# State space phase: the preparation chain of a tile starts two steps earlier, and the gate z is made together with the next tile's conv

## Chip, core and metric

One core of a Trainium2 chip runs the whole kernel in one launch. The metric is the time on the device in microseconds (us) of one execution; the kernel is float32 with a few bf16 operands that stand for exact splits.

## What is computed

The input x is (8, 64, 128, 128). A first layer (attention over the 4096 pooled pixels of each image, layer norm, bilinear upsampling) gives an image of the same size. The second layer, where the change is, is a state space block over the pixels in raster order, all eight images as one sequence of 131072 tokens with 64 channels, 128 inner channels and 16 states:

```python
xz = u @ in_proj_w.T
xh, z = (xz[:, :d_inner], xz[:, d_inner:])
xp = jnp.pad(xh, ((D_CONV - 1, 0), (0, 0)))
conv = conv_b
for k in range(D_CONV):
    conv = conv + xp[k:k + L] * conv_w[:, k]
xc = jax.nn.silu(conv)
dbc = xc @ x_proj_w.T
dt = dbc[:, :dt_rank]
...
delta = jax.nn.softplus(dt @ dt_proj_w.T + dt_proj_b)
A = -jnp.exp(A_log)
def step(h, t):
    d, b, c, xt = t
    h = h * jnp.exp(d[:, None] * A) + (d * xt)[:, None] * b[None, :]
    return (h, h @ c)
...
y = ys + xc * D
y = y * jax.nn.silu(z)
```

Behind it stand two projections, a layer norm over the 64 channels, a silu and the residual sum with u.

## The kernel before

The program has two phases: `attention_phase`, which writes its tokens to `zn_tokens`, and `mamba_phase`, from about 4900 us of the profile on. Only the second is touched. It goes through 256 tiles of 512 tokens (TB), 128 channels on the partitions; state n of a tile is one [128, 512] row of work, and there are S = 16 of them. The order on each engine is written out by hand: a loop body of 16 steps, `step(n)` for n in 14, 15 of tile g and then for n in 0 to 13 of tile g + 1, two tiles (s = 0 and 1) to one pass of the inner loop. Engines meet only by semaphores, and each carries out its own list in order.

What one step holds on each engine:

- **VectorE**: `inputs(n + 1)`, the product of the next state's B row (in one of four PSUM banks `bbank`) with `du` (L904), then the scan of state n (L918).
- **TensorE**: `spread_b(n + 3)` writes the B row of state n + 3 into `bbank` (L1123; it needs the scan of four states earlier), then `add_state(n - 3)` adds a product with C into `ybank` (L1133, `sum_mm`; "add k" below). Step 3 has no add, and step 4 has the skip term (L1131) and adds 0 and 1.
- **ScalarE**: `decay(n + 4)`, the exponential `da` of one state (L1033).
- **GpSimd**: the product `pr` of state n with its C row (L838).

Beside it, `prep(n, tau)` prepares tile g + 2 in fixed steps, and `post(n, g)` finishes tile g. The chain of `prep`, with the step at which it stands before:

- TensorE 0: `ubank` <- u, the upsampling (L1078). ScalarE 1: two short copies of history and two copies of `ubank` to `u2` (L955 to L961).
- TensorE 2: conv, two matmuls into `vbank` (L1084, L1085), and z into `ubank` (L1087). ScalarE 3: `xc`, `sz` (the gate, which waits for `yb` of the tile that used its buffer), and `so` of an earlier tile (L967, L971, L1007), between two loads of an activation table.
- TensorE 5: `vbank` <- `xc` and `ubank` <- `xc` (L1091, L1093). ScalarE 6: `av`, `bcs` (the first part of B and C), `ev`, `ct`, `e1`, `lv`, `ed` (L977 to L993), ScalarE 7: relu (L995).
- TensorE 7: the first remainder, "neg" (L1097); ScalarE 8: `bcs` again (L998, signal `mid_done`; "mid"); TensorE 9: the second remainder, "last" (L1102, waits for `mid_done`); ScalarE 10: the low part (L1001).
- GpSimd 8, 9: `cv` and `l2` (L808, L813). VectorE 11: `dl` (L886), which the decays and `du` of that tile need. GpSimd 12: `du` (L817).

`post` holds: ScalarE 0 `ures` (L1014), VectorE 3 `yb` (L892, after the last add), TensorE 5 `pc` (L1109), ScalarE 6 `sl` (the square, L1018), TensorE 8 the variance (L1114), ScalarE 9 `lnr` and `rs`, VectorE 12 `qn` (L896), GpSimd 6 the residual (L829). On an engine that has both, ScalarE does `post` before `prep`, TensorE `prep` before `post`. SyncE writes the C rows of a tile to memory and loads them back spread over the partitions, and loads the tokens of later tiles.

## Time and profile before

| | us |
|---|---|
| median of 3 runs | 13125.51 (13124.51 to 13127.3) |
| the profiled execution | 13120.83 |
| span of its profile | 13119.0 |

| engine | busy us | share of the span |
|---|---|---|
| TensorE, matmul | 11668.5 | 89% |
| VectorE | 10235.9 | 78% |
| ScalarE | 7905.5 | 60% |
| GpSimd | 7307.1 | 56% |

The shares are means over both phases: in the first VectorE is half idle, and in the second it is over nine tenths busy. So only a view of the second phase tells what bounds it. Matmul ends in the trace are modelled, so that a busy TensorE is not one at its peak.

### The profile page before, as it was taken

Reading aid. Unit: us, or ns where it says so; the run is one execution under the profiler, and the core shown is the slowest. Engines: PE = TensorE matmul, PEld = TensorE weight load, DVE = VectorE, ACT = ScalarE, POOL = GpSimd, SP = SyncE. Lnnn points to the kernel's source line nnn. Section 1 sums busy time; section 2 is a strip of 40 time slices with the busy share of each in tenths; the row PEclk is TensorE's granted clock in tenths of the full one; section 3 lists DMA queues with packets and bytes.
Section 4 is the critical chain, followed back from the end, with each engine's and each line's share of the span. In section 5 each row is a group of like instructions: output and inputs, shape, how many; then the busy total and the mean of one; then the engine's idle time right before and its main releaser. Section 6 shows DMA issues by size and latency. Waiting matters only on the chain.

```text
span 13119.0 us, 161233 instructions
## 1 busy us (share of the span) xinstructions
PE 11668.5 (89%) x34287; PEld 4280.2 (33%) x34287; DVE 10235.9 (78%) x13211; ACT 7905.5 (60%) x12824; POOL 7307.1 (56%) x5412
## 2 busy tenths in 40 slices
PE   4989899999989998888888888888888888888888
PEld 1333333333333333333333333333333333333333
DVE  6454545455454439999999999999999999999999
ACT  1333333333333337777777777777777777777777
POOL 6030303022030007777777777777777777777777
PEclk9989899999989999999999999999999999999999
DMA  2010100101010003333333433333343343333333
GB/s 56 2 27 2 27 9 21 28 2 27 2 27 2 1 10 150 151 144 147 155 144 144 156 146 144 151 151 144 147 155 144 144 155 147 144 152 150 144 149 153
DMA packets 372433, 1297.68 MB, mean 99 GB/s; under 512 B 177904, under 2 KB 177904, under 8 KB 231792
## 3 DMA queue, kind: packets, MB, share of 16 engines
q1 hardware_dynamic: 372336, 1296.81, 26.8%
q14 instruction: 88, 0.72, 0.0%
q8 instruction: 9, 0.15, 0.0%
HBM read 1246.07 MB, written 50.56 MB: 99 GB/s over the span
## 4 chain that ended last, share of the span: by engine, by line
PE 22%; issue 15%; ACT 14%; DVE 9%; POOL 1%; ACTq 0%; DVEq 0%; POOLq 0%; DMA 0%; SPq 0%
PE ybank L1133 7%; ACT da L1033 6%; DVE bbank L904 5%; DVE h L918 3%; PE bbank L1123 2%; PE ubank L1087 2%; PE pbank L1109 2%; PE vbank L1084 2%; PE vbank L1085 2%; PE vbank L1091 2%; PE ubank L1093 2%; PE ybank L1131 2%; ACT av L977 1%; ACT e L989 1%; ACT ev L984 1%
## 5 line engine op out<-in xcount | busy, mean ns | idle before, releaser
L838 POOL TENSOR_TENSOR pr<-h,cc 128x512 f32<-128x512 f32 x4110 | 5201.5, 1269 | 1381.4 <-DVE h L918 1380.1
L918 DVE TENSOR_TENSOR_SCAN h<-da,h,bbank 128x512 f32<-128x512 f32 x4110 | 5198.8, 1265 | 0.0
L1133 PE MATMUL ybank<-pr,m_small 128*128 128x512 f32 x8214 | 4195.6, 597 | 0.0
L904 DVE TENSOR_TENSOR bbank<-bbank,du 128x512 f32<-128x512 f32 x4111 | 2766.5, 673 | 44.6 <-PE bbank L1123 10.0
L432 ACT ACTIVATE prob<-st 128x512 f32<-128x512 f32 x2048 | 1222.7, 597 | 2575.1 <-PE st L564 2575.1
L1033 ACT ACTIVATE da<-dl,a 128x512 f32<-128x512 f32 x4114 | 2736.4, 712 | 17.1 <-DVE dl L886 1.1
L307 DVE TENSOR_REDUCE mpart<-s 128x1 f32<-128x512 f32 x2048 | 1322.2, 686 | 1089.5 <-PE s L530 1081.0
L1123 PE MATMUL bbank<-bcs,selb 96*128 96x512 bf16 x4113 | 1556.5, 389 | 646.7 <-DVE h L918 623.9
L564 PE MATMUL st<-qf,kf 65*128 (+1 forms) x4096 | 2121.3, 620 | 5.9 <-ACT qf L436 5.9
L240 POOL TENSOR_TENSOR rowsum<-xin 128x1024 f32<-128x1024 f32 x64 | 153.5, 2398 | 2994.4 <-PE vb L597 2905.0
L1133 PEld LDWEIGHTS ybank<-pr,m_small 128*128 128x128 f32 x8214 | 1561.0, 194 | 678.7 <-issue 597.6
L1123 PEld LDWEIGHTS bbank<-bcs,selb 96*128 96x128 bf16 x4113 | 375.7, 96 | 2726.1 <-DVE h L918 2209.8
L808 POOL TENSOR_TENSOR cv<-ed,ev 128x512 f32<-128x512 f32 x258 | 327.2, 1268 | 1408.2 <-ACT ed L993 1407.9
L579 PE MATMUL ob<-prob,v 128*64 128x512 f32 x4096 | 1090.5, 616 | 0.0
L564 PEld LDWEIGHTS st<-qf,kf 65*128 65x128 f32 x4096 | 696.5, 190 | 1123.1 <-issue 617.8
L529 PE MATMUL s<-ka,qh 128*128 128x512 bf16 x2048 | 791.5, 386 | 134.6 <-DVE mpart L307 112.3
L530 PE MATMUL s<-ka,qm 128*128 128x512 bf16 x2048 | 787.4, 384 | 0.0
L958 ACT COPY u<-ubank 64x512 f32<-64x512 f32 x258 | 149.4, 579 | 1041.3 <-PE ubank L1078 1041.3
L337 DVE TENSOR_SCALAR zn<-z,mv,rstd 128x64 f32<-128x64 f32 x256 | 62.9, 310 | 912.4 <-ACT rstd L448 912.4
L1018 ACT ACTIVATE sl<-pbank,pbc 64x512 f32<-64x512 f32 x256 | 174.7, 682 | 578.8 <-PE pbank L1109 578.8
L300 DVE SCALAR_TENSOR_TENSOR yc<-xb,dwq,yc (+1 forms) x256 | 455.4, 1779 | 33.3 <-DVE yc L300 23.4
L886 DVE TENSOR_TENSOR dl<-l,vbank 128x512 f32<-128x512 f32 x258 | 177.6, 688 | 349.8 <-issue 330.5
(153 smaller groups left out, 11693.5 us busy)
## 6 DMA issues: line engine op xcount, KB each, us to landing
cc<-c_rows SPq DMA_DIRECT2D x1032, 1024.0 KB, 7.9
upw<-up SPq DMA_DIRECT2D x260, 256.0 KB, 9.5
xin<-x SPq DMA_DIRECT2D x128, 512.0 KB, 6.8
out<-ot SPq DMA_DIRECT2D x256, 128.0 KB, 2.3
zw<-zn_tokens SPq DMA_DIRECT2D x780, 32.0 KB, 9.8
c_rows<-crows SPq DMA_DIRECT2D x258, 32.0 KB, 1.6
zn_tokens<-znb SPq DMA_DIRECT2D x64, 128.0 KB, 2.0
a_small<-small SPq DMA_DIRECT2D x1, 1331.0 KB, 5.6
```

The costliest lines, as they stand in the source:

```text
L307: dve.tensor_reduce(mpart[:, t:t + 1], s1[t % 2][:, :], AX.X, ALU.max).then_inc(s1_max, 1)
L432: act.activation(prob[t % 4][:, :], st[t % 2][:, :], ACT.Exp).then_inc(exp_done, 1)
L529: pe.matmul(s1[t % 2][:, :], qh[:, q], keys, start=True, stop=False)
L530: pe.matmul(s1[t % 2][:, :], qm[:, q], keys, start=False, stop=True).then_inc(s1_mm, 1)
L564: pe.matmul(st[t % 2][:, :], kf[0:C + 1, t * P:t * P + P], q, start=True, stop=True).then_inc(st_mm, 1)
L579: mm = pe.matmul(ob[64 * half:64 * half + 64, :], v[:, k + half, C:2 * C], prob[(k + half) % 4][:, :], start=(k == 0), stop=(k == KT - 2))
L838: pool.tensor_tensor(pr[:, n % 8, :], h[:, n, :], cc[par][:, n, :], ALU.mult).then_inc(prod_done, 1)
L904: dve.tensor_tensor(bbank[n % 4][:, :], bbank[n % 4][:, :], du[par][:, :], ALU.mult)\
L918: dve.tensor_tensor_scan(h[:, n, :], da[:, n % 8, :], bbank[n % 4][:, :], h[:, n, TB - 1:TB], ALU.mult, ALU.add).then_inc(scan_done, 1)
L1033: act.activation(da[:, n % 8, :], dl[par][:, :], ACT.Exp, scale=a[:, n:n + 1]).then_inc(da_done, 1)
L1123: pe.matmul(bbank[n % 4][:, :], selb[:, n, :], bcs[par][:, :], start=True, stop=True)\
L1133: pe.matmul(ybank[:, :], w("ident"), pr[:, n % 8, :], start=False, stop=(n == S - 1))\
```

## The change

`prep` starts two steps earlier, in steps 14 and 15 of the tile before, counted as -2 and -1; the loops call `prep` and `post` there too. TensorE's u matmuls go from 0 to -2, conv from 2 to 0, the `xc` matmuls from 5 to 3, the two remainders from 7 and 9 to 5 and 7. ScalarE's entries go from 1, 3, 6, 7, 8, 10 to -1, 1, 4, 5, 6, 8, GpSimd's `cv` and `l2` from 8, 9 to 6, 7, its `du` from 12 to 11, VectorE's `dl` from 11 to 10, and `ures` from 0 to -2. `sl` stays at 6 and now stands behind the softplus chain. The z matmul of a tile is no longer made with its own conv but with that of the next tile, from the `u2` that is still kept; `sz` is then made for tile tau - 1, waits for a `yb` of a tile earlier, and VectorE's `yb` waits for `sz_done`. The diff, cut to its core:

```diff
@@ gpsimd prep
-                if n == 8:
+                if n == 6:
...
-                if n == 9:
+                if n == 7:
...
-                if n == 12:
+                if n == 11:
@@ vector prep, post
-                if n == 11:
+                if n == 10:
...
+                    dve.wait_ge(sz_done, g + 1)
                     dve.tensor_tensor(yb[:, :], ybank[:, :], sz[s][:, :], ALU.mult).then_inc(yb_done, 1)
@@ scalar prep, post
-                if n == 1:
+                if n == -1:
...
-                if n == 3:
+                if n == 1:
                     act.wait_ge(conv_mm, tau + 1)
                     if not first:
                         act.wait_ge(sum_mm, (tau - 1) * S)
                         act.wait_ge(du_done, tau - 1)
                     act.activation(xc[par][:, :], vbank[:, :], ACT.Silu, bias=w("convb")).then_inc(xc_done, 1)
-                    act.wait_ge(z_mm, tau + 1)
-                    if not first:
-                        act.wait_ge(yb_done, tau - 1)
-                    act.activation(sz[par][:, :], ubank[:, :], ACT.Silu).then_inc(sz_done, 1)
+                    if not start:
+                        act.wait_ge(z_mm, tau)
+                        if not first:
+                            act.wait_ge(yb_done, tau - 2)
+                        act.activation(sz[1 - par][:, :], ubank[:, :], ACT.Silu).then_inc(sz_done, 1)
...
-                if n == 6:
+                if n == 4:
...
-                if n == 7:
+                if n == 5:
...
-                if n == 8:
+                if n == 6:
...
-                if n == 10:
+                if n == 8:
...
-                if n == 0:
+                if n == -2:
                     act.wait_ge(u2_done, g * 2 + 2)
@@ scalar, main loop (the prologues likewise)
                         for n in range(K, S):
                             step(n, g, s, False)
+                            post(n - S, g, s)
+                            prep(n - S, g + 2, s, b * PAIRS + i + s + 1, False, False)
@@ tensor prep
-                if n == 0:
+                if n == -2:
...
-                if n == 2:
+                if n == 0:
...
-                    pe.matmul(ubank[:, :], w("inT")[0:64, P:2 * P], u2[par][0:64, 2:2 + TB], start=True,
-                              stop=True).then_inc(z_mm, 1)
-                if n == 5:
+                    if not start:
+                        pe.matmul(ubank[:, :], w("inT")[0:64, P:2 * P], u2[1 - par][0:64, 2:2 + TB], start=True,
+                                  stop=True).then_inc(z_mm, 1)
+                if n == 3:
...
-                    pe.wait_ge(sz_done, tau + 1)
+                    pe.wait_ge(sz_done, tau)
...
-                if n == 7:
+                if n == 5:
...
-                if n == 9:
+                if n == 7:
```

How it moves the instructions of one tile shows in the programs as built. The semaphores in brackets are those for which an instruction waits. First ScalarE around `xc`, in the loop body. Before:

```order
L958 COPY u<-ubank 64x512 [waits u_mm]
L961 COPY u<-ubank 64x512 [waits hist_done]
L1032 REGISTER_ALU
L1033 ACTIVATE da<-dl,a 128x512 [waits scan_done] x2
L967 ACT_TABLE_LOAD [waits du_done,sum_mm]
L967 ACTIVATE xc<-vbank,m_small 128x512 [waits conv_mm]
L971 ACTIVATE sz<-ubank 128x512 [waits yb_done,z_mm]
L1007 ACTIVATE so<-qn,m_small 64x512 [waits add_done,qn_done]
L974 ACT_TABLE_LOAD
```

Of the change:

```order
L959 COPY u<-ubank 64x512 [waits u_mm]
L962 COPY u<-ubank 64x512 [waits hist_done]
L1034 REGISTER_ALU
L1035 ACTIVATE da<-dl,a 128x512 [waits scan_done]
L1034 REGISTER_ALU
L1035 ACTIVATE da<-dl,a 128x512 [waits scan_done]
L968 ACT_TABLE_LOAD [waits du_done,sum_mm]
L968 ACTIVATE xc<-vbank,m_small 128x512 [waits conv_mm]
L973 ACTIVATE sz<-ubank 128x512 [waits yb_done,z_mm]
L1009 ACTIVATE so<-qn,m_small 64x512 [waits add_done,qn_done]
L976 ACT_TABLE_LOAD
```

Two decays stand between the copies of u and the table load in both; the load carries the waits for `du_done` and `sum_mm`, and `xc` the one for `conv_mm`. What moved lies in the loop's steps: the group is two steps earlier than before.

TensorE around conv, in the second tile of the loop body; `sum_mm` is counted up by the rows `ybank<-pr` (L1133, in the change L1140). Before, from the B row of state 4 to the one of state 5 (the first row is state 4's):

```order
L1123 MATMUL bbank<-bcs,selb 128x512 [waits scan_done]
L1132 REGISTER_ALU
L1133 MATMUL ybank<-pr,m_small 128x512 [waits prod_done]
L1082 ISA
L1084 MATMUL vbank<-u,tapw 128x512 [waits dl_done,u2_done]
L1085 MATMUL vbank<-u,tapw 128x512
L1087 MATMUL ubank<-u,m_small 128x512
L1122 REGISTER_ALU
L1123 MATMUL bbank<-bcs,selb 128x512 [waits scan_done]
```

Of the change, from behind add 13 to add 15 (its last row):

```order
L1088 ISA
L1090 MATMUL vbank<-u,tapw 128x512 [waits dl_done,u2_done]
L1091 MATMUL vbank<-u,tapw 128x512
L1094 MATMUL ubank<-u,m_small 128x512
L1129 REGISTER_ALU
L1130 MATMUL bbank<-bcs,selb 128x512 [waits scan_done]
L1139 REGISTER_ALU
L1140 MATMUL ybank<-pr,m_small 128x512 [waits prod_done]
L1129 REGISTER_ALU
L1130 MATMUL bbank<-bcs,selb 128x512 [waits scan_done]
L1139 REGISTER_ALU
L1140 MATMUL ybank<-pr,m_small 128x512 [waits prod_done]
```

The convs and z stood behind add 15; now they stand in front of add 14 and add 15.

TensorE around the second remainder ("last", the row that waits for `mid_done`). Before, from the B row of state 11 to add 7:

```order
L1123 MATMUL bbank<-bcs,selb 128x512 [waits scan_done]
L1133 MATMUL ybank<-pr,m_small 128x512 [waits prod_done]
L1114 MATMUL pbank<-sl,m_small 64x512 [waits sq_done,rs_done]
L1122 REGISTER_ALU
L1123 MATMUL bbank<-bcs,selb 128x512 [waits scan_done]
L1133 MATMUL ybank<-pr,m_small 128x512 [waits prod_done]
L1102 MATMUL ubank<-bcs,neg 32x512 [waits mid_done]
L1122 REGISTER_ALU
L1123 MATMUL bbank<-bcs,selb 128x512 [waits scan_done]
L1133 MATMUL ybank<-pr,m_small 128x512 [waits prod_done]
```

Of the change, from the B row of state 10 to add 6:

```order
L1130 MATMUL bbank<-bcs,selb 128x512 [waits scan_done]
L1140 MATMUL ybank<-pr,m_small 128x512 [waits prod_done]
L1109 MATMUL ubank<-bcs,neg 32x512 [waits mid_done]
L1129 REGISTER_ALU
L1130 MATMUL bbank<-bcs,selb 128x512 [waits scan_done]
L1140 MATMUL ybank<-pr,m_small 128x512 [waits prod_done]
L1121 MATMUL pbank<-sl,m_small 64x512 [waits sq_done,rs_done]
L1129 REGISTER_ALU
L1130 MATMUL bbank<-bcs,selb 128x512 [waits scan_done]
L1140 MATMUL ybank<-pr,m_small 128x512 [waits prod_done]
```

The row behind `last` was that of state 13 and is that of state 11. ScalarE's part of the same place, from the first decay behind the softplus chain to `mid` (the row that waits for `rest_mm`). Before, and then of the change:

```order
L1033 ACTIVATE da<-dl,a 128x512 [waits scan_done]
L995 ACTIVATE vbank<-vbank,m_small 128x512
L1032 REGISTER_ALU
L1033 ACTIVATE da<-dl,a 128x512 [waits scan_done]
L998 CAST bcs<-ubank 64x512 [waits rest_mm]
```

```order
L1035 ACTIVATE da<-dl,a 128x512 [waits scan_done]
L997 ACTIVATE vbank<-vbank,m_small 128x512
L1034 REGISTER_ALU
L1035 ACTIVATE da<-dl,a 128x512 [waits scan_done]
L1020 ACTIVATE sl<-pbank,pbc 64x512 [waits var_mm,pc_mm]
L1000 CAST bcs<-ubank 64x512 [waits rest_mm]
```

The square `sl` now stands between the second of these decays and `mid`.

## Rows read from the trace of the kernel before

**Rows 1.** Busy us (count) of PE, PEld, DVE, ACT, POOL; granted clock; DMA share; GB/s.

```profile
8000.00:10000.00 2000.00, 1754.76 (x4896) 651.24 (x4896) 1906.52 (x2198) 1525.78 (x2451) 1571.57 (x1256) 0.99 0.39 149
```

**Rows 2.** `dl` (L886): first and last start, idle before it; 5000 to 13000.

```profile
L886 DVE TENSOR_TENSOR dl<-l,vbank x251: 686/689/690, 5022.6 to 12981.3; 128x512 f32<-128x512 f32 x126
...
  issue: 324.0, 251
```

**Rows 3.** Timeline, VectorE: start, duration, line, count, idle before and its end.

```profile
8085.84 1.26 DVE L918 TENSOR_TENSOR_SCAN h<-da,h,bbank 128x512 f32<-128x512 f32 x1
8087.03 0.67 DVE L904 TENSOR_TENSOR bbank<-bbank,du 128x512 f32<-128x512 f32 x1
...
8100.60 1.26 DVE L918 TENSOR_TENSOR_SCAN h<-da,h,bbank 128x512 f32<-128x512 f32 x1
8101.99 0.70 DVE L904 TENSOR_TENSOR bbank<-bbank,du 128x512 f32<-128x512 f32 x1
...
8105.56 0.67 DVE L904 TENSOR_TENSOR bbank<-bbank,du 128x512 f32<-128x512 f32 x1
...
8110.55 0.69 DVE L886 TENSOR_TENSOR dl<-l,vbank 128x512 f32<-128x512 f32 x1 [1.37 <-issue]
...
8117.72 1.26 DVE L918 TENSOR_TENSOR_SCAN h<-da,h,bbank 128x512 f32<-128x512 f32 x1
```

**Rows 4.** Timeline, GpSimd, the second softplus operation.

```profile
8109.18 1.28 POOL L813 TENSOR_TENSOR l<-lv,cv 128x512 f32<-128x512 f32 x1
```

**Rows 5.** Timeline, ScalarE, the same tile.

```profile
8092.04 1.28 ACT L967 ACT_TABLE_LOAD   x1
...
8094.86 0.60 ACT L971 ACTIVATE sz<-ubank 128x512 f32<-128x512 f32 x1 [0.47 <-DVE yb L892]
...
8097.46 1.95 ACT L1033 ACTIVATE da<-dl,a 128x512 f32<-128x512 f32 x3
8101.67 0.68 ACT L1018 ACTIVATE sl<-pbank,pbc 64x512 f32<-64x512 f32 x1 [2.26 <-PE pbank L1109]
8102.25 0.67 ACT L977 ACTIVATE av<-vbank,m_small 128x512 f32<-128x512 f32 x1
...
8106.33 0.71 ACT L1033 ACTIVATE da<-dl,a 128x512 f32<-128x512 f32 x1
8107.06 0.66 ACT L995 ACTIVATE vbank<-vbank,m_small 128x512 f32<-128x512 f32 x1
...
8108.26 0.57 ACT L998 CAST bcs<-ubank 64x512 bf16<-64x512 f32 x1
```

**Rows 6.** Timeline, TensorE, the same tile.

```profile
8089.36 0.39 PE L1123 MATMUL bbank<-bcs,selb 96*128 96x512 bf16 x1
8089.59 1.02 PE L1133 MATMUL ybank<-pr,m_small 128*128 128x512 f32 x2
...
8090.93 1.02 PE L1133 MATMUL ybank<-pr,m_small 128*128 128x512 f32 x2
8091.79 1.02 PE L1084 MATMUL vbank<-u,tapw 128*128 128x512 f32 x2
...
8093.60 1.12 PE L1087 MATMUL ubank<-u,m_small 64*128 64x512 f32 x2
8094.65 0.60 PE L1123 MATMUL bbank<-bcs,selb 96*128 96x512 bf16 x2
...
8101.56 0.39 PE L1123 MATMUL bbank<-bcs,selb 96*128 96x512 bf16 x1
...
8108.97 0.37 PE L1102 MATMUL ubank<-bcs,neg 32*32 32x512 bf16 x1 [1.38 <-ACT bcs L998]
8109.27 0.39 PE L1123 MATMUL bbank<-bcs,selb 96*128 96x512 bf16 x1
```

**Rows 7.** Timeline, ScalarE, the first table load of the second phase.

```profile
4912.25 1.28 ACT L942 ACT_TABLE_LOAD   x1 [12.50 <-DMA selb<-sel]
```

**Rows 8.** The same table, where the second phase begins.

```profile
4900.00:4925.00 25.00, 9.73 (x27) 4.50 (x27) 4.29 (x20) 4.63 (x6) 0.00 (x0) 0.51 0.34 106
```

More of the change, by code:

```diff
@@ L1039, in step @@
                     decay(n + LEAD - S, g + 1, 1 - par, False)
-            for n in range(K):
+            for n in range(-2, K):
                 prep(n, 0, 0, None, True, True)
@@ L1044, in _ @@
                 decay(n, 0, 0, True)
+            for n in (-2, -1):
+                prep(n, 1, 1, 1, False, True)
             for n in range(K):
@@ L1068, in _, with prep @@
             pe.wait_ge(ini_v, 14)
-            def prep(n, tau, par, count):
-                if n == 0:
+            def prep(n, tau, par, count, start=False):
+                if n == -2:
                     pe.wait_ge(zw_in[par], count * 64)
@@ L1148, in step @@
                     add_state(n - LAG + S, g - 1)
-            for n in range(K):
-                prep(n, 0, 0, 1)
+            for n in range(-2, K):
+                prep(n, 0, 0, 1, True)
             for n in range(AHEAD):
                 spread_b(n, 0, 0, True)
+            for n in (-2, -1):
+                prep(n, 1, 1, 1)
             for n in range(K):
@@ L1162, in _ @@
                             step(n, g, s, False)
+                            prep(n - S, g + 2, s, b * PAIRS + i + 2)
                         for n in range(K):
```

## The prediction

> **What bounds the kernel now.** I read the views from coarse to fine. The busy table of a long stretch of the second phase comes first [rows 1]: VectorE is busy 1906.52 of 2000 us, no other engine is over 1755, and TensorE's granted clock is 0.99, its 2.4 GHz level. So VectorE sets the pace, and the question is what is left of its idle time. The line of `dl` [rows 2] has 251 starts from 5022.6 to 12981.3, which is a **tile period** of 7958.7 / 250 = 31.835 us, and 324.0 us idle ahead of it, 1.29 us each. The loop runs 256 such tiles, so 0.1 us in each tile is 25.6 us.
>
> Then one tile in order of time. I set a clock to zero where the scan of state 15 ends, R = 8085.84 + 1.26 = 8087.10 [rows 3]; the next R is 8117.72 + 1.26 = 8118.98, and this tile took 31.88. The operation behind a scan normally starts 1.19 after it, 0.07 before the scan's end (8085.84, 8087.03). `dl` starts after an idle time of 1.37, so it is held 1.44 in all. What holds it is GpSimd's `l2`, which starts 8109.18 and takes 1.28 [rows 4]: it ends 0.09 before `dl` starts at 8110.55. The view puts the wait down to issue, which is how this chain looks when its last link sits on GpSimd. Upstream, ScalarE waited 2.26 us for `pc` before it could begin `sl`, `av` and the rest of the softplus chain [rows 5]. A second, smaller loss of 0.2: TensorE writes the B row of state 9 at 8101.56 and VectorE takes it 0.43 later at 8101.99 [rows 3, 6], where 8100.60 + 1.19 = 8101.79 was possible.
>
> **What the change takes away.** `dl` goes one step earlier, all in front of it two steps earlier. `sl` no longer stands in front of `av`. `sz` loses its 0.47 us wait for `yb` [rows 5]. If nothing else came in, `dl` would not wait: gain (1.29 + 0.07) x 256 = 348 us. No instruction is added or taken away; the time is decided by where the queues stand.
>
> **What the change brings: three queues worked through again,** all times after R, spacings from the rows.
>
> *TensorE* [rows 6]. The u matmuls move to before R, two steps of a queue that has some 0.7 us to spare in each (a row and an add take 0.23 + 0.86 of 1.78, the half of 8105.56 - 8101.99), so TensorE has caught up when R comes. At R + 0.06 it writes the row of state 3 (the 0.06 is an estimate that the next rows don't depend on much), 0.23 later add 13, 0.86 later conv. Two convs and z now follow at once: conv to z is 8093.60 - 8091.79 = 1.81, z to the next row 1.05. Only then come row 4, add 14, row 5, add 15: 0.06 + 0.23 + 0.86 + 1.81 + 1.05 = 4.01; + 0.23 + 0.86 + 0.23 = 5.33 for the start of **add 15**; it lasts 1.02 and ends at 6.35. The 0.23 is row to add (8089.36, 8089.59), the 0.86 add to conv (8090.93, 8091.79).
>
> *ScalarE* [rows 5]. The order shows what the diff doesn't: the wait for `sum_mm` (add 15 of the tile before last) is not on the `xc` activation but on the **table load** in front of it. In before this costs nothing: the load starts at 8092.04, when add 15 (8090.93 + 1.02) has just ended, and the activation then waits for conv anyway. Now conv is ready at 0.06 + 0.23 + 0.86 + 0.86 + 1.02 = 3.03, but the load may not start before 6.35. That a table load is held by its waits is in the trace at the phase's start: one sat 12.50 us for a DMA [rows 7]. The signal to the load takes at most 8092.04 - 8091.95 = 0.09; I take 0.05. So: load 6.40; `xc` 7.69 (the load's 1.28 and 0.01); `sz` 8.27 (0.58, as `sl` to `av`); decays 6, 7, 8 from 10.87 (`sz` to the first decay is 8097.46 - 8094.86 = 2.60, with `so` and the second load in it), 0.62 each (1.95 for three, the last 0.71); `av` at 10.87 + 1.24 + 0.73 = 12.84, where 0.73 is the step from a decay to an activation with a bias (8106.33, 8107.06). The smaller step, 0.62, would give 12.73. `av` to decay 9 is 8106.33 - 8102.25 = 4.08: 16.92. From there to `mid` took 8108.26 - 8106.33 = 1.93; now `sl` stands between decay 10 and `mid`, + 0.58, and the step into it is 0.73 for 0.62: 2.62, so **`mid` starts at 19.54**.
>
> *TensorE again.* `last` moves from step 9 to step 7 of its queue, and the row behind it is now that of state 11 instead of 13. `last` starts 8108.97 - 8108.26 = 0.71 after `mid`, the row 0.30 later, VectorE 0.43 after that [rows 3, 5, 6]: 19.54 + 0.71 + 0.30 + 0.43 = **20.98 for VectorE's product of state 11**. In before this product started at 8105.56, 18.46 after R, of which 0.2 was the loss at state 9; so the new wait is 20.98 - 18.26 = 2.7 us. It takes the place of the 1.44 at `dl` and the 0.2 at state 9. Part of it falls earlier, since TensorE stands still for `xc` until about 8.5: rows 8 and 9 come late by about 0.5 and 0.7. This changes nothing in the sum, since the chain that ends at 20.98 starts at R and runs over ScalarE. Queued behind the waiting `last` are row 11, add 5, the variance matmul and row 12; VectorE waits for the rows.
>
> The rest of the tile: from the product of state 11 to the next R is 8118.98 - 8105.56 = 13.42, less the 1.44 held at `dl`, 11.98. Is `dl` free? GpSimd does state 6, the residual, `cv` (from 17.1, when `ed` is done), state 7 and `l2`, operations of 1.28 and less, done by about 20.9; `dl` is due at 20.98 + 0.59 + 1.19 = 22.8, a slack of 1.9. Row 12 comes 2.2 after row 11 and is due 2.4 after it. The decays hold nobody: decay 6 ends at 11.6 and scan 6 starts at 11.7, the tightest of them; decay 9 ends at 17.6 for 18.3. SyncE's queue: the write of the C rows waits for `ct` (about 15.1) and stands behind the output of the tile before, which waits for the residual at about 15.5. Its tile is more than a period away: no cost.
>
> **Sum.** New period 20.98 + 11.98 = 32.96 against 31.835: + 1.12 us, x 256 = + 287 us. The profiled execution took 13120.83 us (span 13119.0), so 13408; the runs shown have a median 4.7 us higher, 13125.51. Forecast: **13412 us, slower by 2.2%**. Bounds of what the trace doesn't show: the signal to a held load (0.05 as taken, up to the 0.43 from TensorE to VectorE: + 100 us at most, of which I allow half), the two steps of 0.62 or 0.73 (- 0.22: - 56 us). So 13350 to 13465 for this case, 13310 to 13490 with what a dozen spacings may hide.
>
> On the load itself the row shows 1.28 us [rows 7], and 2.60 us hold a `sz`, a `so` and a load [rows 5]. The Trainium skill, "ScalarE: Activation LUTs", section "What ACT_TABLE_LOAD costs", gives the same 1.28 but adds a drain of 1.38 to every switch. With that drain exposed behind the held load the sum would be 1.38 x 256 = 353 us higher, an estimate from that page; there is no room for it in the 2.60, and I don't count it.
>
> **Rivals.**
> - *The load isn't in the way* (it starts ahead of its wait, or add 15 comes early enough to hide it). For: in before it never visibly waited in the loop. Against: the 12.50 us of [rows 7]. The chain is 1.29 shorter, the period 31.67, - 0.17: **13082**. The sign turns when at least 1.12 of the 1.29 is hidden. Chance 0.10.
> - *The change does what it says*: `dl` stops waiting and no other wait comes. - 348: **12778**. Against: `last` would have to start by R + 17.5, 2.7 before my sum. Chance 0.03.
> - *The two sides cancel* within 0.2%: needs the product of state 11 between 19.76 and 19.96. Chance 0.03.
> - *TensorE's clock falls.* Its idle stretches grow to about 2 us (for `xc`) and 2.5 (for `mid`), from 1.38 at `last` [rows 6]. At the phase's start, where TensorE was busy 9.73 of 25 us, the clock was granted at 0.51, the 1.2 GHz level [rows 8]. If one tile in ten ran at this level, its 28 us of matmuls (1754.76 in 62.8 tiles) would take double: 26 x 24 = + 620, **14030**. Against: the loop's waits of 1.38 left it at 0.99 [rows 1]. The Trainium skill, "TensorE: Matmul & The Clock Gate", section "HAM oscillation — how this bites in real kernels", warns of kernels in which every pause re-throttles the array; no row of this loop shows that. Chance 0.04.
>
> **How the numbers follow.** The main case has 0.80, nearly all of it within 13310 to 13490; the range is 13290 to 13510, which leaves about 0.2 out. Faster by over 0.2% (26 us, about what a measurement here can tell from no change): the first two rivals, 0.13. Within 0.2%: 0.03. Slower: 0.84.
>
> **What would show it.** (1) `dl` with no idle before it, and the `bbank` products with about 2.7 us of waits a tile, put down to TensorE's `bbank` rows. (2) The first table load with about 4 us idle before it, until R + 6.4. (3) `last` at R + 20.2, TensorE idle some 2.5 us for `bcs` before it. (4) `sz` without its wait for `yb`. (5) A period near 33.0. I am wrong if the load starts near R + 2, if the wait before `last` is under 1 us, or if the clock of the loop is under 0.98.

## Result and profile after

The changed kernel takes **13709.72 us** (median of 4 runs, 13706.55 to 13714.89) against 13125.01 of the kernel before in the same runs: the ratio is 1.0446, with a 95% interval of 1.0428 to 1.0464. It is 585 us or 4.5% slower. The forecast was slower by 2.2%, 13412 us, in a range of 13290 to 13510: the sign was right, and the size half of what came. All runs behind the numbers here and below ran alike but one of `a_fill`'s four, which took 29198.08 us at a mean clock of 0.40 for a cause that stays open; without it the median of `a_fill` is 13347.36 and not 13348.57.

The first thing to look at is the busy table of a long stretch of the second phase. Of the change, and then of the kernel before, over the same stretch (the columns are those of [rows 1]):

```profile
6000.00:12000.00 6000.00, 5275.56 (x13704) 1962.68 (x13703) 5385.51 (x6154) 4213.17 (x6860) 4397.93 (x3517) 0.92 0.36 138
```

```profile
6000.00:12000.00 6000.00, 5267.26 (x14697) 1955.46 (x14697) 5724.45 (x6597) 4581.95 (x7355) 4718.55 (x3772) 0.99 0.39 148
```

VectorE has gone from 5724 to 5386 busy us in 6000, and nobody else has taken over: TensorE's busy time is the same. But its granted clock is 0.92 and not 0.99. The table of who waited for whom, change, same stretch (waiting engine and line, releaser, us in total, times, longest):

```profile
ACT L968 <- issue: 882.7, 176, 5.0
...
DVE bbank L905 <- PE bbank L1130: 612.4, 694, 2.0
...
PE vbank L1098 <- ACT xc L968: 332.4, 176, 1.9
...
PE ubank L1109 <- ACT bcs L1000: 231.7, 176, 2.1
```

Against [rows 2], `dl` isn't in this list: its 205 starts from 5508.1 to 12470.1 have no idle before them, and they give the new period, 6962.0 / 204 = 34.13 us against 31.84. In its place VectorE waits 612.4 us in 176 tiles, 3.5 a tile, for B rows of TensorE. The table load of ScalarE, which wasn't in the list before, is held 882.7 us or 5.0 a tile. TensorE waits 1.9 for `xc` and up to 2.1 at `last`; before it was 1.38 at `last` alone [rows 6]. The wait of `sz` for `yb` [rows 5] is gone, since z is ready long before the late `xc`.

One tile in order of time. Its clock starts where the scan of state 15 ends, R = 8111.13 + 1.26 = 8112.39. VectorE:

```profile
8111.13 1.26 DVE L919 TENSOR_TENSOR_SCAN h<-da,h,bbank 128x512 f32<-128x512 f32 x1
...
8125.87 0.70 DVE L905 TENSOR_TENSOR bbank<-bbank,du 128x512 f32<-128x512 f32 x1 [0.40 <-PE bbank L1130]
...
8128.39 0.70 DVE L905 TENSOR_TENSOR bbank<-bbank,du 128x512 f32<-128x512 f32 x1 [0.64 <-PE bbank L1130]
...
8133.48 0.70 DVE L905 TENSOR_TENSOR bbank<-bbank,du 128x512 f32<-128x512 f32 x1 [1.45 <-PE bbank L1130]
...
8135.28 0.66 DVE L886 TENSOR_TENSOR dl<-l,vbank 128x512 f32<-128x512 f32 x1
8137.62 0.70 DVE L905 TENSOR_TENSOR bbank<-bbank,du 128x512 f32<-128x512 f32 x1 [1.68 <-PE bbank L1130]
...
8146.22 1.26 DVE L919 TENSOR_TENSOR_SCAN h<-da,h,bbank 128x512 f32<-128x512 f32 x1
```

ScalarE in the same tile, from the first table load to `mid` (L1000):

```profile
8118.80 1.28 ACT L968 ACT_TABLE_LOAD   x1 [5.03 <-issue]
8120.10 0.69 ACT L968 ACTIVATE xc<-vbank,m_small 128x512 f32<-128x512 f32 x1
...
8125.13 0.67 ACT L979 ACTIVATE av<-vbank,m_small 128x512 f32<-128x512 f32 x1
...
8130.52 0.71 ACT L1035 ACTIVATE da<-dl,a 128x512 f32<-128x512 f32 x1
8131.13 0.67 ACT L1020 ACTIVATE sl<-pbank,pbc 64x512 f32<-64x512 f32 x1
8131.70 0.57 ACT L1000 CAST bcs<-ubank 64x512 bf16<-64x512 f32 x1
```

TensorE at `last` (L1109):

```profile
8132.41 0.49 PE L1109 MATMUL ubank<-bcs,neg 32*32 32x512 bf16 x1 [2.12 <-ACT bcs L1000]
...
8133.24 1.91 PE L1140 MATMUL ybank<-pr,m_small 128*128 128x512 f32 x2
8135.08 1.97 PE L1121 MATMUL pbank<-sl,m_small 64*64 64x512 f32 x2
8136.98 0.61 PE L1130 MATMUL bbank<-bcs,selb 96*128 96x512 bf16 x1
...
8139.44 1.02 PE L1140 MATMUL ybank<-pr,m_small 128*128 128x512 f32 x2
```

The load starts at R + 6.41 (the forecast had 6.40), after 5.03 us of idle time; `xc` at 7.71 (7.69), `av` at 12.74, `mid` at 19.31 (19.54), `last` at 20.02 and VectorE's product of state 11 at 21.09 (20.98). `dl` follows at 8135.28 without a wait. The two waits of 0.40 and 0.64 are those for rows 8 and 9, which stand behind the late v matmul. So far the tile runs as written down. Then it leaves the forecast: the add behind row 11 takes 1.91 us for its two passes and not 1.02, the variance matmul 1.97, row 12 0.61 for 0.39 (at 8139.44 an add takes 1.02 again), and VectorE, which should have had the product of state 12 at 8135.86, waits until 8137.62. From product 11 to the next R (8146.22 + 1.26 = 8147.48) it is 14.0 us, where the forecast took 11.98. The busy table around it, two stretches of 8 us:

```profile
8124.00:8132.00 8.00, 6.29 (x16) 2.03 (x14) 6.96 (x8) 7.83 (x14) 5.93 (x5) 1.00 0.12 28
8132.00:8140.00 8.00, 7.59 (x12) 2.44 (x13) 4.73 (x7) 5.44 (x10) 5.42 (x6) 0.57 1.00 407
```

The clock was at its full 2.4 GHz level until the pause of 2.12 us before `last`, and for most of the next 8 us at the 1.2 GHz level (0.57 in the mean). This tile took 35.09 us.

It is one of two kinds. The next tile has R = 8147.48, and there the clock falls behind the pause for `xc`; TensorE's queue is then late, so that little is left of the pause at `last`, and the clock stays up behind it:

```profile
8155.92 1.61 PE L1098 MATMUL vbank<-xc,wdl 128*128 128x512 f32 x2 [1.89 <-ACT xc L968]
...
8167.50 0.37 PE L1109 MATMUL ubank<-bcs,neg 32*32 32x512 bf16 x1 [0.44 <-ACT bcs L1000]
```

```profile
8156.00:8160.00 4.00, 4.00 (x6) 1.72 (x7) 2.99 (x4) 3.97 (x6) 2.41 (x2) 0.57 0.00 0
```

```profile
8168.73 0.67 DVE L905 TENSOR_TENSOR bbank<-bbank,du 128x512 f32<-128x512 f32 x1
...
8179.41 1.27 DVE L919 TENSOR_TENSOR_SCAN h<-da,h,bbank 128x512 f32<-128x512 f32 x1
```

`last` is on time at R + 20.02, VectorE's product of state 11 starts at R + 21.25, and the tile takes 8179.41 + 1.27 - 8147.48 = 33.20. Counted over the whole stretch from 6000 to 12000, every tile has one stretch of low clock: in 92 it begins behind the pause at `last`, and these take 34.98 us in the mean, in the others behind the pause for `xc`, and these take 33.20. In the mean 5.2 us of a tile are at the 1.2 GHz level.

### The profile page after: what moved, and what is told of

Same layout as the page of the kernel before. It is cut to its first block, busy times and chain, and to the rows that moved or that the text cites. A ratio compares the mean times of both kernels' runs of the same rounds, so it can differ in the third digit from the quotient of the medians.

```text
span 13713.1 us, 161052 instructions
## 1 busy us (share of the span) xinstructions
PE 12193.3 (89%) x34109; PEld 4484.8 (33%) x34285; DVE 10302.8 (75%) x13211; ACT 7816.4 (57%) x12823; POOL 7304.6 (53%) x5412
## 4 chain that ended last, share of the span: by engine, by line
DVE 17%; issue 16%; PE 16%; ACT 13%; DVEq 1%; ACTq 0%; POOL 0%; DMA 0%; POOLq 0%; SPq 0%
DVE bbank L905 9%; PE ybank L1140 6%; ACT da L1035 5%; DVE h L919 5%; PE bbank L1130 2%; PE pbank L1121 2%; PE ubank L1100 1%; PE vbank L1098 1%; ACT L976 1%; DVE yb L893 1%; PE ybank L1138 1%; DVE qn L897 1%; PE pbank L1116 1%; ACT so L1009 1%; ACT xc L968 1%
## 5 line engine op out<-in xcount | busy, mean ns | idle before, releaser
L1140 PE MATMUL ybank<-pr,m_small 128*128 128x512 f32 x8214 | 4415.9, 625 | 0.0
L1140 PEld LDWEIGHTS ybank<-pr,m_small 128*128 128x128 f32 x8214 | 1659.3, 204 | 969.4 <-issue 623.6
L1130 PE MATMUL bbank<-bcs,selb 96*128 96x512 bf16 x4113 | 1693.4, 412 | 230.8 <-DVE h L919 209.2
L1130 PEld LDWEIGHTS bbank<-bcs,selb 96*128 96x128 bf16 x4113 | 411.0, 100 | 2203.0 <-DVE h L919 1247.2
L529 PE MATMUL s<-ka,qh 128*128 128x512 bf16 x1872 | 724.6, 387 | 110.5 <-DVE mpart L307 108.7
L1098 PE MATMUL vbank<-xc,wdl 128*128 128x512 f32 x516 | 336.4, 737 | 484.3 <-ACT xc L968 484.3
```

What stands on the lines that cost most here:

```text
L529: pe.matmul(s1[t % 2][:, :], qh[:, q], keys, start=True, stop=False)
L1130: pe.matmul(bbank[n % 4][:, :], selb[:, n, :], bcs[par][:, :], start=True, stop=True)\
L1140: pe.matmul(ybank[:, :], w("ident"), pr[:, n % 8, :], start=False, stop=(n == S - 1))\
```

## The experiments

Twelve kernels were run, all beside the kernel before on the same chip; the medians are of four runs or more. "Clock" is the granted clock from 6000 to 12000 us, "period" the mean distance of the starts of `dl`.

| kernel | median us | against before (95%) | clock | period us |
|---|---|---|---|---|
| before | 13122 to 13125 | | 0.99 | 31.84 |
| the change | 13709.72 | 1.0446 (1.0428 to 1.0464) | 0.92 | 34.13 |
| a_relax | 12701.97 | 0.9679 (0.9663 to 0.9695) | 1.00 | 30.20 |
| a_preload | 13321.34 | 1.015 (1.0133 to 1.0167) | 0.93 | 32.66 |
| a_fill | 13348.57 | 1.017 (1.015 to 1.0191) | 1.00 | 32.74 |
| b_relax | 13121.84 | 1.0 (0.999 to 1.0009) | 0.99 | 31.85 |
| a_prefill | 13020.72 | 0.9921 (0.9905 to 0.9938) | 1.00 | 31.45 |
| a_sl | 13464.92 | 1.0259 (1.0242 to 1.0277) | 0.95 | 33.16 |
| b_gap | 13152.73 | 1.0022 (1.0013 to 1.0032) | 0.95 | 31.97 |
| b_z | 13122.02 | 0.9999 (0.9989 to 1.0008) | 0.99 | 31.85 |
| a_fill_xc | 13731.62 | 1.046 (1.0443 to 1.0478) | 0.93 | 34.23 |
| a_fill_mid | 13707.82 | 1.0445 (1.0427 to 1.0462) | 0.95 | 34.13 |
| a_half | 13348.52 | 1.0171 (1.0154 to 1.0188) | 1.00 | 32.73 |
| a_last9 | 13037.25 | 0.9933 (0.9916 to 0.9949) | 1.00 | 31.51 |

**Is it the held table load that makes the chain late?** `a_relax` changes one number of the change: the wait ahead of `xc` asks for the skip term of the tile that last used the buffer, not for its add 15.

```diff
                     if not first:
-                        act.wait_ge(sum_mm, (tau - 1) * S)
+                        act.wait_ge(sum_mm, (tau - 2) * S + 1)
                         act.wait_ge(du_done, tau - 1)
```

> The change, with one number altered: the wait ahead of xc asks for the skip term and add 0 of the tile before last (sum_mm of (tau - 2) * 16 + 1) in place of its add 15. The skip term is the last reader of that xc buffer on TensorE, so the order of the data is kept. Theory H (the table load held until add 15 starts a chain load, xc, softplus, mid, last, row 11 that ends after VectorE needs it): the load starts near R + 1.4, xc near R + 3.1, mid near R + 16, no row comes late, dl doesn't wait, TensorE's clock is back at 0.99: a period of 30.3 us and about 12725 us (12690 to 12790). Rival Q (the new places in TensorE's queue, convs and z ahead of rows 4 and 5 and last ahead of row 11, cost the time by themselves): still above 13400.

Measured: 12701.97 us, 1008 us below the change and 420 below the kernel before. The busy table, the wait that is left on VectorE, and ScalarE's timeline in a tile with R = 8106.83:

```profile
6000.00:12000.00 6000.00, 5462.93 (x15489) 2073.49 (x15488) 5994.95 (x6955) 4777.27 (x7753) 4967.66 (x3975) 1.00 0.41 156
```

```profile
DVE bbank L905 <- PE bbank L1130: 4.5, 9, 0.5
```

```profile
8110.04 1.28 ACT L968 ACT_TABLE_LOAD   x1 [1.80 <-PE vbank L1091]
...
8122.95 0.57 ACT L1000 CAST bcs<-ubank 64x512 bf16<-64x512 f32 x1
```

VectorE is busy 5995 of 6000 us and waits 4.5; the clock is 1.00. The load shown starts at R + 3.2 and not R + 1.4: in 99 of 198 tiles it waits for conv, since the compiled program hangs another of the waits on it there; this has slack. `mid` is at R + 16.1, as expected. Rival Q has fallen: the new places in TensorE's queue cost nothing when the chain starts on time. The same number in the kernel before does nothing, which shows that the hold is a product of the change:

> The kernel before, with the same relaxed wait ahead of xc. Theory H: in before the load isn't held, since it starts when the decays ahead of it are done and xc then waits for conv: 13125 within 15 us. Rival: the hold was already there in before and hidden by the coincidence of the two times; then up to 30 us faster.

Measured: 13121.84 us against 13122.35, ratio 1.0 (0.999 to 1.0009).

**How much of it is the load itself?** `a_preload` writes the load ahead of the waits, so that only `xc` is held:

```diff
                 if n == 1:
+                    act.preload_act_table_set("silu_and_others")
                     act.wait_ge(conv_mm, tau + 1)
```

> The change, with the load of the silu table set written ahead of the three waits, so that the load is free to start and xc itself waits for add 15. Theory H: xc starts at R + 6.4 and not 7.7, everything behind it 1.3 us earlier, product 11 near R + 19.8, TensorE's two waits about 0.6 and 0.9 us and too short to cost it clock: 13060 to 13130. Rival C (the clock falls at any new wait of TensorE, however short): the clock stays near 0.92 and the time above 13350. Rival Q: no change from 13710.

Measured: 13321.34 us, a gain of 388 us on the change, but no clock: 0.93. The wait for `xc` is the 0.61 us that was expected, the one at `last` is not 0.9 but 2.12 as before, since the queue ahead of `last` moved forward with the chain. That was a mistake in my expectation, and a lucky one, as it leaves one long pause in a tile whose times are otherwise known. TensorE:

```profile
8112.45 0.37 PE L1110 MATMUL ubank<-bcs,neg 32*32 32x512 bf16 x1 [2.12 <-ACT bcs L1001]
...
8113.94 1.90 PE L1122 MATMUL pbank<-sl,m_small 64*64 64x512 f32 x2
```

The variance matmul behind the pause takes 1.90 us, the next add (8116.17) 1.91. Neither theory as written held here; the next ones were made to part the chain from the clock.

**The price of the clock.** `a_fill` gives TensorE matmuls to do that nobody reads, at the two places where it stands idle (the same code with 9 ahead of `last`):

```diff
                 if n == 3:
+                    if loop:
+                        pe.wait_ge(rs_done, tau - 2)
+                        pe.sem_inc(pe_passed, 1)
+                        for _ in range(8):
+                            pe.matmul(pbank[64:128, :], selb[0:64, 0, 0:64], selb[0:64, 0:4, :], start=True, stop=True)
                     pe.wait_ge(xc_done, tau + 1)
```

> The change, with matmuls that nobody reads (bf16, 64x64 on 512 columns, into the free half of pbank) ahead of the two waiting matmuls: 8 ahead of the v matmul, 9 ahead of last, about 0.22 us each, as much as TensorE stands idle there. Theory H + clock (of the 2.3 us per tile some 1.2 come from the chain and 1.1 from the lowered clock): granted clock back at 0.99 or more, a period of 33.1 us, about 13440 us (13400 to 13490). Rival (the low clock costs nothing by itself, it only shows where TensorE has time): 13700 or more, since the fillers take nothing off the chain.

Measured: 13348.57 us with the clock at 1.00, 361 us less than the change although nothing was taken off the chain. The tile with R = 8107.95, VectorE:

```profile
8123.95 0.70 DVE L905 TENSOR_TENSOR bbank<-bbank,du 128x512 f32<-128x512 f32 x1 [0.64 <-PE bbank L1140]
...
8128.72 0.70 DVE L905 TENSOR_TENSOR bbank<-bbank,du 128x512 f32<-128x512 f32 x1 [1.12 <-PE bbank L1140]
...
8130.52 0.66 DVE L886 TENSOR_TENSOR dl<-l,vbank 128x512 f32<-128x512 f32 x1
...
8139.43 1.27 DVE L919 TENSOR_TENSOR_SCAN h<-da,h,bbank 128x512 f32<-128x512 f32 x1
```

The wait of 0.64 for row 9 stays, and `dl` comes without a wait at 8130.52. Product 11 starts at R + 20.77 and the next R (8139.43 + 1.27 = 8140.70) is 11.98 later: a period of 32.75 in this tile, 32.74 in the mean. This is the forecast's sum with its smaller step (0.62 and not 0.73) at both places: 20.98 - 0.22 = 20.76, and 11.98. At full clock the chain costs 32.74 - 31.84 = 0.90 us a tile, and 13348.57 - 13122.35 = 226 us in all.

> The change with the table load free to start ahead of the waits (as in a_preload) and 9 unread matmuls ahead of last, where TensorE stood idle 2.12 us in a_preload. Both costs of theory H + clock but for the plain lateness of the chain are out: product 11 near R + 19.48, period 31.45, 13025 us (13000 to 13060), granted clock 0.99 or more. Rival (the 0.6 us wait for xc that is left also costs clock): above 13150.

`a_prefill` is `a_preload` with the 9 matmuls ahead of `last`. Measured: 13020.72 us, a period of 31.45, clock 1.00. Without the load in the chain and with the clock held, the sum of durations (13025) gives the time to 5 us. It also prices the clock in `a_preload`: 301 us.

**Which pause lowers the clock?** One filler at a time:

> The change with only the 8 unread matmuls ahead of the v matmul, where TensorE waits 1.89 us for xc. The wait of 2.12 us at last stays. Theory H + clock, with either wait enough to lower the clock: between a_fill (13349) and the change (13710), 13500 to 13650, clock 0.93 to 0.96; a_preload had the same two waits at 0.6 and 2.12 us and lost about 300 us to the clock, so I take 13640. If only the wait for xc mattered: 13349.

> The change with only the 9 unread matmuls ahead of last; the wait of 1.89 us for xc stays. Theory H + clock: a_sl, whose wait at last was 1.55, lost about 250 us to the clock, so 13500 to 13620 here, clock 0.94 to 0.97. If only the wait at last mattered: 13349.

Measured: 13731.62 and 13707.82 us, so one filler alone gives back nothing of the time. The remaining pause in each, and the matmuls behind it (L1114 is `last` in `a_fill_xc`, L1098 the v matmul in `a_fill_mid`):

```profile
8104.71 0.37 PE L1114 MATMUL ubank<-bcs,neg 32*32 32x512 bf16 x1 [2.12 <-ACT bcs L1000]
...
8105.24 1.71 PE L1145 MATMUL ybank<-pr,m_small 128*128 128x512 f32 x2
8106.88 1.97 PE L1126 MATMUL pbank<-sl,m_small 64*64 64x512 f32 x2
```

```profile
8113.10 1.50 PE L1098 MATMUL vbank<-xc,wdl 128*128 128x512 f32 x2 [1.89 <-ACT xc L968]
8114.39 1.91 PE L1100 MATMUL ubank<-xc,m_small 128*128 128x512 f32 x2
...
8124.17 2.13 PE L1111 MATMUL pbank<-selb 64*64 64x512 bf16 x9
8126.23 0.38 PE L1114 MATMUL ubank<-bcs,neg 32*32 32x512 bf16 x1
```

Both show the 1.2 GHz durations behind their pause (1.71 and 1.97, 1.50 and 1.91 for two passes). So either pause alone is enough to lower the clock, though not every time: behind 129 of 175 pauses in `a_fill_xc`, behind 158 of 175 in `a_fill_mid`. I had expected shares of the time (13640 and 13500 to 13620); both lie outside.

The two times look like one price for either pause, but the tiles say otherwise. In `a_fill_xc` those with a low clock take 34.76 us in the mean and the 46 without 32.72, as in `a_fill`: about 2 us a tile, lost behind `last`. In `a_fill_mid` they are 34.29 and 32.73, and most of this 1.56 is the fillers' own doing. The rows of `a_fill_mid` above are of the tile with R = 8104.65. The low clock behind `xc` makes the queue late, TensorE comes to `last` only when `mid` is nearly done, and the 9 unread matmuls find no idle time to fill: they run for 2.13 us from 8124.17, `last` starts at R + 21.58 and not at R + 20.02, and the product of state 11 follows at R + 22.32:

```profile
8126.97 0.70 DVE L905 TENSOR_TENSOR bbank<-bbank,du 128x512 f32<-128x512 f32 x1 [0.98 <-PE bbank L1135]
```

The change itself has tiles with the same low clock behind `xc` and no fillers, and they lose 33.20 - 32.74 = 0.46 us, so that 1.09 of the 1.56 are left to the fillers. Those whose clock falls behind `last` lose 34.98 - 32.74 = 2.24. Over 256 tiles the two kinds together give the 361 us. The run nearest to the pause for `xc` alone is `a_sl` below.

> The change with about half of the unread matmuls at both places (4 and 5), so that both waits of TensorE are left at about 1.0 us. If the length of a single pause decides: before had 1.38 us and a clock of 0.99, so the clock is 0.99 and the time that of a_fill, 13349 within 30 us. Rival (any idle time costs clock in proportion): about 13530, clock 0.95.

With 4 and 5 matmuls the pauses are about 0.9 us each, and the waits say so:

```profile
PE ubank L1119 <- ACT bcs L1000: 171.8, 184, 0.9
PE vbank L1103 <- ACT xc L968: 166.8, 183, 0.9
```

Measured: 13348.52 us, the same as `a_fill`, clock 1.00. So idle time as such is not what costs; 1.8 us of it in a tile, in two pieces, left the clock up, and 1.89 in one piece lowered it in nine tiles of ten (`a_fill_mid`). The rival of a price in proportion has fallen.

`a_sl` puts the square behind `mid`, which shortens the chain and the second pause but not the first:

```diff
-                            post(n, g, s)
-                            prep(n, g + 2, s, b * PAIRS + i + s + 1, False, False)
+                            if n == 6:
+                                prep(n, g + 2, s, b * PAIRS + i + s + 1, False, False)
+                                post(n, g, s)
+                            else:
+                                post(n, g, s)
+                                prep(n, g + 2, s, b * PAIRS + i + s + 1, False, False)
```

> The change with the square sl behind mid instead of ahead of it on ScalarE (step 6), nothing else. Theory H: mid 0.57 us earlier, the chain ends 0.57 earlier (32.17 us a tile at full clock, 13211 us), TensorE's wait at last 1.55 us and the one for xc still 1.89. With the clock falling only at the wait for xc: 13250 to 13500 and a clock between 0.93 and 0.97. Rival (only the wait at last lowers the clock): 13211 within 30 us and a clock of 0.99.

Measured: 13464.92 us, clock 0.95: inside the range of the first theory, 254 us above the 13211 that the sum gives at full clock. Its own trace bears this sum out: 48 tiles without a low stretch take 32.16 us in the mean, where the sum has 32.17. It fits with the pause of 1.89 alone being enough: the clock fell behind 128 of 181 of these pauses, `last` has a pause of up to 1.56 in 53 tiles only, and no fillers stand here.

**Does a pause do it in the kernel before, too?** `b_gap` holds `mid` back there by two copies into a scratch tile, where the sum says that the delay itself is free:

```diff
                 if n == 8:
                     act.wait_ge(rest_mm, tau + 1)
+                    act.copy(gapt[0:64, :], ubank[0:64, :])
+                    act.copy(gapt[64:128, :], ubank[64:128, :])
                     act.copy(bcs[par][0:64, :], ubank[0:64, :]).then_inc(mid_done, 1)
```

> The kernel before, with two copies of ubank into a scratch tile on ScalarE ahead of mid: mid comes about 0.95 us later, so TensorE stands idle 2.3 us and not 1.38 ahead of last. The row of state 13 behind it is then ready 0.5 us before VectorE needs it, and the chain to dl isn't touched, so the delay itself costs nothing. Theory clock (a wait of about 2 us of TensorE, once per tile, is enough for the clock to fall for a while): granted clock in the loop under 0.96 and some 50 to 300 us slower. Rival (the clock of the changed kernel fell for another reason, or a low clock there costs nothing): clock 0.99 and 13122 within 20 us.

```profile
PE ubank L1105 <- ACT bcs L1001: 481.7, 188, 2.6
...
DVE bbank L905 <- PE bbank L1126: 23.3, 65, 0.7
```

Measured: 13152.73 us, ratio 1.0022 (1.0013 to 1.0032), clock 0.95, pause 2.56 us (481.7 in 188 tiles). The clock falls here as well, with not one instruction of the changed order present. But it costs 29 us and not 360, under the 50 that I had named as the lower end. VectorE waits 23.3 us in this stretch for B rows where it had waited 7 in the kernel before. The 44 tiles without a low stretch take 31.81 us in the mean, as in the kernel before, and the 143 with one 32.01: the delay itself is free, and the 29 us are the clock's. My reading is that the rows behind `last` have more slack there, and that a low clock costs what the queue behind the pause can't make up; this was only argued, not tested by itself.

**Where `last` stands.** `a_last9` puts `last` back in step 9 and its reader on ScalarE back in step 10, with the 8 unread matmuls of `a_fill` ahead of the v matmul to hold the clock:

```diff
@@ tensor prep
-                if n == 7:
+                if n == 9:
                     pe.wait_ge(mid_done, tau + 1)
@@ scalar prep
-                if n == 8:
+                if n == 10:
                     act.wait_ge(last_mm, tau + 1)
```

> The change with last back in step 9 of TensorE's queue and the low part of B and C back in step 10 of ScalarE's, as in before, and the 8 unread matmuls ahead of the v matmul to keep the clock; the held table load stays. Theory H (the wait for mid costs because rows 11 and 12 stand behind last): rows 11 and 12 are written before the wait and only the lateness of rows 8 and 9 behind the late v matmul is left, about 1.2 us a tile on 30.2: 31.4 to 31.7 us a tile, 13020 to 13100, and dl still unheld. Rival Q (the late chain costs wherever last stands): 13349.

```profile
ACT L968 <- issue: 955.5, 190, 5.0
...
DVE bbank L905 <- PE bbank L1135: 197.3, 380, 0.6
```

Measured: 13037.25 us, with the load held as before (955.5 us in 190 tiles, 5.0 each) and `dl` without a wait. `a_fill` differs from it in the place of `last` and its reader, and in the 9 unread matmuls ahead of `last`, and takes 311 us more: the late chain is harmful above all because rows 11 and 12 stand behind `last`. What is left, 197.3 us in 190 tiles or 1.0 a tile, is rows 8 and 9 behind the late v matmul. Even with its held load the change would have been faster than the kernel before (0.9933, 0.9916 to 0.9949), had `last` stayed where it was and the clock held.

**The z part alone,** in the kernel before:

```diff
-                    act.wait_ge(z_mm, tau + 1)
-                    if not first:
-                        act.wait_ge(yb_done, tau - 1)
-                    act.activation(sz[par][:, :], ubank[:, :], ACT.Silu).then_inc(sz_done, 1)
+                    if not start:
+                        act.wait_ge(z_mm, tau)
+                        if not first:
+                            act.wait_ge(yb_done, tau - 2)
+                        act.activation(sz[1 - par][:, :], ubank[:, :], ACT.Silu).then_inc(sz_done, 1)
```

> The kernel before with only the z part of the change: z and its gate are made one tile later from the kept u, sz no longer waits for yb of the running tile, yb waits for sz_done. Theory H: the 0.47 us that ScalarE gains there it gives back in its wait of 2.26 us for pc, so 13122 within 15 us. Rival: the chain to dl starts 0.47 earlier and the tile is up to 0.4 us shorter, 13020.

Measured: 13122.02 us, ratio 0.9999 (0.9989 to 1.0008). The edit takes away less than I thought: over the stretch `sz` waits 68.6 us (58.0 put down to `yb`, 10.6 to z) where it waited 86.7, since z's own matmul is ready hardly sooner than `yb` was (before, 8093.60 + 1.12 against 8094.11 + 0.66). What is gained, 18.1 us, is given back at the wait for `pc`, which grows from 427.3 to 445.6 us.

## Why the prediction was right and wrong

- **What bounds the kernel, and what the change takes away: right.** VectorE sets the pace, and the 1.44 us at `dl` were to be had. `a_relax` took all of it and the 0.2 at state 9: a period of 30.20, where 31.84 - 1.44 - 0.2 = 30.2. The 1.44 is of one tile; with the mean of the loop, 1.29 + 0.07 = 1.36, the sum is 30.28, and 0.08 isn't accounted for.
- **The held table load: right.** Start R + 6.41 for 6.40, and `a_relax` shows that the slowdown goes with that one wait. This could be seen only in the built order, where `sum_mm` stands on the load.
- **The wait moves from `dl` to the row behind `last`: right,** product 11 at R + 21.09, at full clock 20.77 (`a_fill`) for 20.98. The step from a decay to an activation with a bias is 0.61 here (8130.52, 8131.13), not 0.73; this is - 56 us, which the bounds had.
- **The size of the chain: nearly right.** + 287 us forecast, 226 measured at full clock.
- **TensorE's clock: the step that failed.** The forecast saw the pauses of 2 and 2.5 us coming (1.89 and 2.12 were measured), had the mechanism as its fourth rival, and gave it 0.04. The sentence that carried this was "the loop's waits of 1.38 left it at 0.99": it took a row about a shorter pause as evidence on a longer one. Nor was that row clean. The 0.99 is a mean: from 6000 to 12000 the clock of the kernel before falls for a moment in 20 of 189 tiles, and 12 of these moments begin within half a microsecond of the end of the 1.38 pause. They cost nothing there (31.83 us a tile with and without), so they could be seen only in a table of short stretches:

```profile
8299.78 0.37 PE L1102 MATMUL ubank<-bcs,neg 32*32 32x512 bf16 x1 [1.38 <-ACT bcs L998]
```

```profile
8300.00:8304.00 4.00, 4.00 (x8) 1.68 (x8) 2.64 (x4) 3.89 (x7) 3.81 (x5) 0.57 1.01 420
```

No row of the loop showed a pause of 2 us, which called for both ends of the range: full clock, and a clock lowered in each tile. The price was mis-set too: one tile in ten wholly at 1.2 GHz, + 620 us. What happens is a low clock in every tile, for 5.2 us in the mean, and it costs 361 us (13709.72 - 13348.57). The prediction's own sign of being wrong, a clock of the loop under 0.98, is what came (0.92). With the term in, the sum is 287 + 361 = 648, against 585 measured.
- **The page on the clock,** "TensorE: Matmul & The Clock Gate" of the Trainium skill, section "HAM oscillation — how this bites in real kernels", was cited and set aside because no row showed it. The traces agree with its warning that pauses of TensorE re-throttle the array: each run of the loop with a pause of 1.89 us or more had a mean clock of 0.92 to 0.95. They don't agree that it is every pause: behind the 1.89 us for `xc` the clock fell in 84 of 176 tiles of the change.
- **The drain behind a table load: rightly left out.** In the change `xc` starts 1.30 us after its load (8118.80, 8120.10). The second load of that tile, which isn't held, starts at 8121.98, 0.01 after the end of `so`, and the next decay at 8123.28, again 1.30 later. With the clock held, the sum with 1.28 for the held load meets the time of `a_fill` within 8 (13125.51 + 0.90 x 256 = 13356). `a_prefill` says nothing on this, since its first load isn't in the chain.
- **The rivals of the faster side** didn't come about in the change itself, but `a_relax` is just what the second one said (12778 forecast, 12701.97 measured; of the 76 us between them 51 are the 0.2 at state 9, and the rest isn't accounted for).

## What to carry to other kernels

When a step is moved earlier in a hand-written order, walk through every queue with the waits as the built program carries them: a wait may sit on a helper instruction ahead of the one it was written for, and what stood ahead of its releaser on another engine may now stand behind. A wait for the reuse of a buffer should name its last reader; here, asking for the skip term and not for the last add made a 4.5% loss into a 3.2% gain. And when a change makes TensorE wait longer in one piece than anything in the trace before, carry a lowered clock as a term of the sum, not as a remote rival; a few matmuls that nobody reads show in one run what it costs. They do so only where they fit into idle time in every tile; in `a_fill_mid` they didn't, and made most of the loss themselves.

## What the runs showed of the hardware

- Once per tile of 32 to 34 us, a single pause of TensorE of 1.89 to 2.56 us went with a mean clock of 0.92 to 0.95 in the loop; pauses of 0.9 twice (`a_half`), 1.07 (`a_relax`) and 1.38 (before) left it at 0.99 to 1.00.
- A pause doesn't lower the clock every time: the one of 1.38 did in 12 of 189 tiles (before), that of 1.89 in 84 of 176 (the change) and 158 of 175 (`a_fill_mid`), that of 2.56 in 143 of 188 (`b_gap`).
- What a fall costs depends on where it comes: nothing in the kernel before, 0.46 us behind the pause for `xc` and 2.24 behind the one at `last` in the change.
- A mean clock of 0.95 cost 29 us in `b_gap` and 254 in `a_sl`: the mean clock alone doesn't give the time that is lost. That it depends on the slack of what stands behind the pause is my reading, not tested by itself.
- An activation table load is held by the semaphores that the built program puts on it (5.03 us in the change), and the activation behind it starts 1.30 after its start (8118.80, 8120.10).
